# Rounding of the quantized activations moved from VectorE to ScalarE, 8 cores

## The chip, the cores and the metric

One Trainium2 chip, all 8 NeuronCores. The batch of 16 sequences is split over the cores, two sequences for each, and every core runs the same program on its own data without talking to the others. The metric is the device time in microseconds of the slowest core.

## The reference

One transformer layer of the post-norm kind with 1024 features, 16 heads and sequences of 2048 tokens. The feed-forward part is one matrix product on activations that are quantized to 8 bits.

```python
_d["L0_attn_x"]: (16, 2048, 1024) f32
...
scores = jnp.einsum('bhqd,bhkd->bhqk', Q, K) / jnp.sqrt(jnp.float32(dk))
scores = jnp.where(causal, scores, NEG)
m = jnp.max(scores, axis=-1, keepdims=True)
e = jnp.exp(scores - m)
attn = e / jnp.sum(e, axis=-1, keepdims=True)
out = jnp.einsum('bhqk,bhkd->bhqd', attn, V)
...
return out @ WO.T
...
ms = jnp.mean(jnp.square(x), axis=-1, keepdims=True)
x_norm = x * jax.lax.rsqrt(ms + EPS_RMS)
absmax = jnp.max(jnp.abs(x_norm), axis=-1, keepdims=True)
scale = 127.0 / jnp.clip(absmax, EPS_ACT, None)
x_q = jnp.clip(jnp.round(x_norm * scale), -128.0, 127.0) / scale
...
return jnp.einsum('bsd,od->bso', x_q, w_deq) + bias
...
x = _layernorm(x + _L0_attn_ref(x, L0_attn_WQ, L0_attn_WK, L0_attn_WV, L0_attn_WO), axis=-1)
x = _layernorm(x + _L0_ffn_ref(x, L0_ffn_w_int8, L0_ffn_weight_scale, L0_ffn_bias), axis=-1)
```

The part that matters here is `jnp.round`. The kernel does it by adding RC = 12582912 (1.5 times 2 to the 23rd) in f32 and taking it away again: at that size an f32 has no fraction bits, so the first addition rounds to a whole number.

## The kernel before

The kernel is written with an explicit queue for each engine. Functions append instructions and waits on semaphores to the lists of TensorE (PE, "t"), VectorE (DVE, "v"), ScalarE (ACT, "s"), GpSimd (POOL, "g") and SyncE (SP, "y"). Each engine runs its list in the order in which it was written, so an instruction that waits holds up all that stands behind it on that engine.

Each core handles its two sequences one after the other (`b` = 0, 1), in three stages:

- `ph1`: projections. Q and K are computed from the transposed input (matmuls L280, copied out by ACT at L290). V follows in groups at L325.
- `ph2`: causal attention. Scores (L388), exponential on ACT (L489 and L500), mask on POOL (L514), product with V (L406), normalization on DVE (L564) and transposes of the result (L432, L443).
- `ph45`: output projection, first norm, quantization, feed-forward product, second norm. It runs over 16 tiles of 128 tokens by 1024 features, in a software pipeline that is written out by hand. This is the stage of the change.

The steps of `ph45` for a tile t, by their names in the code:

- `emit_wo(t)`: 16 matmuls (L648) of the output projection into `psall`. `emit_xdma(t)` loads the residual into `xstg`.
- `VA(t)`, DVE: adds the residual (L678, z), takes maximum and minimum (L686, L689), mean and variance (L692 to L695), and a row of very small instructions on one column (L698 to L724).
- `SA(t)`, ACT: seven very small instructions (L733 to L751) that turn these into scales.
- `SB(t)`, ACT: writes the normalized tile `x1` in bf16 (L760).
- `VC(t)`, DVE: three passes over the tile: scale (L772, into `x1b`), round by adding RC and -RC (L777, in place), limit to -128..127 and write bf16 (L780, into `qint`).
- `G_x1pb(t)`, POOL: x1 plus bias into `x1b` (L790), after the quantization has read it.
- `T_qt_ffn(t)`: PE transposes `qint` (L803), ACT copies the result out (L816, `qT`), PE runs the 16 matmuls of the feed-forward product (L832).
- `VD(t)`, DVE: combines the product with x1 plus bias (L849), mean and variance (L857 to L870).
- `SD(t)`, ACT: two very small instructions (L882, L885) and the final norm (L889, `outst`). `G_out(t)`, POOL, issues the store (L902).

First come `emit_wo` of tiles 0 to 3, then tiles 0 and 1 with VA, SA, SB, VC, G_x1pb and T_qt_ffn, then VA and SA of tiles 2 and 3. After that the main loop runs for i = 0 to 15:

```python
VD(i)
...
if i + 4 < NP: emit_wo(i + 4)
SD(i, gps[i][0]); G_out(i, gps[i][0])
if i + 2 < NP: SB(i + 2); VC(i + 2); G_x1pb(i + 2); T_qt_ffn(i + 2)
if i + 4 < NP: ...; VA(i + 4, *gps[i + 4]); SA(i + 4)
```

So iterations 0 to 11 hold all steps, 12 and 13 have no new tile for `emit_wo` and `VA`, and 14 and 15 only finish. The accumulator of `emit_wo(i + 4)` is that which VD(i) has just read, so PE waits for L849 of VD(i).

During the `ph45` of the first sequence POOL also issues the loads for the second one (`preload_cb`). Behind VD(13) stand WQ (L965) and 7/8 of the input (L975); they wait for the feed-forward product of tile 13, and in POOL's queue they stand behind G_x1pb(14). Behind VD(15) stand WK (L984) and the rest of the input (L994). The `ph1` of the second sequence needs all of the input before its first matmul.

Of the kernel before, what the change touches and what calls it, by code (L numbers as in the profile page):

```python
# [10 lines left out]
AF = mybir.ActivationFunctionType  # L11
ALU = mybir.AluOpType
# [6 lines left out]
RC = 12582912.0  # L19
# [19 lines left out]
def build_nc():  # L39
# [13 lines left out]
    with ExitStack() as ctx:  # L53
# [27 lines left out]
        def small(name, shape, dtype):  # L81
            nonlocal o
            t = at(name, shape, dtype, o)
            nbytes = shape[1] * {F32: 4, BF16: 2, I32: 4}[dtype]
            o += (nbytes + 31) // 32 * 32
            return t
# [8 lines left out]
        rcol = small("rcol", [128, 1], F32)  # L95
        nrcol = small("nrcol", [128, 1], F32)
# [22 lines left out]
        sem_s = e(nc.semaphore("sem_s"))  # L119
        sem_v = e(nc.semaphore("sem_v"))  # L120
# [16 lines left out]
        def emit(engine, fn):  # L137
            ops[engine].append(fn)

        def bump(key, n=1):  # L140
            ctr[key] += n
            return ctr[key]

        def W(engine, key, val):
            if val is None or val <= 0:
                return
            sem = SEM[key]
            emit(engine, lambda eng, sem=sem, val=val: eng.wait_ge(sem, val))
# [442 lines left out]
        def ph45(b, trans_done, wo_done, w8_done, gpair, exp_last,  # L591
# [13 lines left out]
            ffnv = {}  # L605
            stats2v = {}
            appd2 = {}
            NP = 16

            def bufP(t):  # L610
# [2 lines left out]
            def zq(t):  # L613
                zt = z2 if (t % 4) < 2 else z2x
                return zt[:, (t % 2) * 1024:((t % 2) + 1) * 1024]
# [4 lines left out]
            def x1b2h(t):  # L620
                return x1b2[:, (t % 2) * 1024:((t % 2) + 1) * 1024]

            def qih(t):
                return qint2[:, (t % 2) * 1024:((t % 2) + 1) * 1024]
# [32 lines left out]
            def emit_xdma(t):  # L657
                gp = gpair[0]
                gpair[0] += 1
                W("y", "v", gpair[1].get(gp - 2))  # L660
                key = "xd" if t % 2 == 0 else "xd2"
                sem_x = SEM[key]
                def fd(eng, t=t, b=b, sem_x=sem_x):
                    src = ap(x_h, b * S * D + t * 128 * D, (D, 128), (1, D))
                    eng.dma_start(xh(t), src).then_inc(sem_x, 16)
                emit("y", fd)
                return gp, key, bump(key, 16)
# [61 lines left out]
            def SA(t):  # L729
                W("s", "v", statv[t])  # L730
                c0 = 14 * (t % 4)
                def f4(eng, t=t, c0=c0):
                    eng.activation(sc[:, c0 + 9:c0 + 11],  # L733
                                   sc[:, c0 + 2:c0 + 4], AF.Sqrt)
                    eng.activation(sc[:, c0 + 11:c0 + 12],
                                   sc[:, c0 + 1:c0 + 2], AF.Sqrt)
                    eng.drain()
                    eng.activation(sc[:, c0 + 6:c0 + 7],
                                   sc[:, c0 + 8:c0 + 9], AF.Identity,
                                   scale=sc[:, c0 + 9:c0 + 10])  # L740
                    eng.activation(sc[:, c0 + 7:c0 + 8],
                                   sc[:, c0 + 10:c0 + 11], AF.Identity,
                                   scale=127.0)
                    eng.activation(sc[:, c0 + 13:c0 + 14],
                                   sc[:, c0 + 11:c0 + 12], AF.Identity,
                                   scale=sc[:, c0 + 9:c0 + 10])
                    eng.drain()
                    eng.activation(sc[:, c0 + 12:c0 + 13],
                                   sc[:, c0 + 8:c0 + 9], AF.Identity,
                                   scale=sc[:, c0 + 7:c0 + 8])  # L750
                    eng.activation(w2a[:, t:t + 1],  # L751
                                   sc[:, c0 + 13:c0 + 14], AF.Identity,
                                   scale=wsb127[:, :]).then_inc(sem_s, 1)
                emit("s", f4)
                rsd[t] = bump("s")

            def SB(t):
                c0 = 14 * (t % 4)
                def f6(eng, t=t, c0=c0, z=zq(t)):
                    eng.activation(  # L760
                        x1[:, t * 1024:(t + 1) * 1024], z[:, :],
                        AF.Identity, bias=sc[:, c0 + 6:c0 + 7],
                        scale=sc[:, c0 + 9:c0 + 10]).then_inc(sem_s, 1)
                emit("s", f6)
                appd[t] = bump("s")

            def VC(t):
                W("v", "s", rsd[t])
                W("v", "t", qtmm_v.get(t - 2))
                c0 = 14 * (t % 4)  # L770
                def f7(eng, t=t, c0=c0, z=zq(t)):
                    eng.tensor_scalar(x1b2h(t), z[:, :],  # L772
                                      sc[:, c0 + 7:c0 + 8],
                                      sc[:, c0 + 12:c0 + 13],
                                      ALU.mult, ALU.add)
                    eng.drain()
                    eng.tensor_scalar(x1b2h(t), x1b2h(t), RC, -RC,  # L777
                                      ALU.add, ALU.add)
                    eng.drain()
                    eng.tensor_scalar(qih(t), x1b2h(t), 127.0,  # L780
                                      -128.0, ALU.min,
                                      ALU.max).then_inc(sem_v, 1)
                emit("v", f7)
                qv[t] = bump("v")

            def G_x1pb(t):
                W("g", "s", appd[t])
                W("g", "v", qv[t])
                def fg2(eng, t=t):
                    eng.tensor_tensor(x1b2h(t),  # L790
                                      x1[:, t * 1024:(t + 1) * 1024],
                                      bias_b2[:, 0:1024],
                                      ALU.add).then_inc(sem_m, 1)
                emit("g", fg2)
                x1pbv[t] = bump("g")
# [79 lines left out]
            def SD(t, gp):  # L875
                W("s", "v", stats2v[t])
                if gp >= 2:
                    _ok, _ov = outv[gp - 2]
                    W("s", _ok, _ov)
                c2 = 56 + 5 * (t % 2)  # L880
                def f15(eng, t=t, c2=c2, z=zq(t)):
                    eng.activation(sc[:, c2 + 2:c2 + 3],  # L882
                                   sc[:, c2 + 1:c2 + 2], AF.Sqrt)
                    eng.drain()
                    eng.activation(sc[:, c2 + 4:c2 + 5],  # L885
                                   sc[:, c2 + 3:c2 + 4], AF.Identity,
                                   scale=sc[:, c2 + 2:c2 + 3])
                    eng.drain()
                    eng.activation(  # L889
                        outst2[:, (t % 2) * 1024:(t % 2) * 1024 + 1024],  # L890
                        z[:, :], AF.Identity, bias=sc[:, c2 + 4:c2 + 5],
                        scale=sc[:, c2 + 2:c2 + 3]).then_inc(sem_s, 1)
                emit("s", f15)
                outrd[t] = bump("s")
# [18 lines left out]
            for t in range(2):  # L913
                gps[t] = emit_xdma(t)
                VA(t, *gps[t])
                SA(t)
                SB(t)
                VC(t)
                G_x1pb(t)
                T_qt_ffn(t)  # L920
            for t in (2, 3):
                gps[t] = emit_xdma(t)
                VA(t, *gps[t])
                SA(t)
            for i in range(NP):
                VD(i)
                if preload_cb is not None and i in (13, 15):
                    preload_cb(i, wo_y2v, ffnv)
                if i + 4 < NP:
                    emit_wo(i + 4)  # L930
                SD(i, gps[i][0])
                G_out(i, gps[i][0])
                if i + 2 < NP:
                    SB(i + 2)
                    VC(i + 2)
                    G_x1pb(i + 2)
                    T_qt_ffn(i + 2)
                if i + 4 < NP:
                    gps[i + 4] = emit_xdma(i + 4)
                    VA(i + 4, *gps[i + 4])  # L940
                    SA(i + 4)
# [8 lines left out]
        for b in range(BPC):  # L950
# [7 lines left out]
            def preload_cb(i, wo_y2v, ffnv, nxt=nxt, bn=b + 1):  # L958
# [19 lines left out]
                else:  # L978
# [19 lines left out]

            cb = preload_cb if b + 1 < BPC else None
            ph45(b, trans_done, wo_done, w8_done, gpair, exp_last,  # L1000
                 trans_ev, cb)
            pre = nxt if b + 1 < BPC else None
# [69 lines left out]
```

## Time and profile before

| | before |
|---|---|
| median of 3 runs | 1719.62 us (1715.51 to 1782.61) |
| profiled execution | 1719.22 us |
| its span (core 2, the slowest of 8) | 1717.6 us |
| spans of all cores | 1696.7 to 1717.6 us |
| busy: PE / ACT / DVE / POOL | 1242.3 / 831.5 / 575.8 / 306.0 us |

In all rows times count in microseconds from the start of the span. `ph45` runs from 626 to 854 for the first sequence and from about 1483 to the end for the second. In the rows the name `x1b` stands for the buffer x1b2, `z` and `z2x` for the two buffers of z, `x` for x1, and `128x1 f32` for the very small instructions on one column. A timeline row holds start, duration, engine, line, operation, output and input, and in brackets the idle time ahead of it and what ended it. A row of the windows holds the stretch, its length, the busy time (and the number of instructions) of PE's matmuls, PE's weight loads, DVE, ACT and POOL, then the granted clock of TensorE as a share of 2.4 GHz, the busy share of the DMA engines and the GB/s that they moved.

### The profile page before, as it was taken

The numbers are of one execution on the slowest core, as the hardware profiler recorded it, in microseconds if no ns is written. First come the engines' busy times: TensorE is split into PE (matmuls) and PEld (weight loads), VectorE is DVE, ScalarE is ACT, GpSimd is POOL, SyncE is SP. The second block draws the span as 40 slices with busy tenths as digits, with TensorE's granted clock in tenths as the row PEclk, the third lists the DMA queues.
The fourth block names the chain that finished last, engine by engine and source line by source line (L and its number), as shares of the span: only waits on it lengthen the run. The fifth ranks groups of instructions, "written<-read, shape, count | busy, mean of one in ns | idle before, by whom it ended". The sixth has DMA issues, their size and how long they took to land.

```text
span 1717.6 us, 25253 instructions; the slowest of 8 cores (1696.7 to 1717.6 us)
## 1 busy us (share of the span) xinstructions
PE 1242.3 (72%) x8710; PEld 586.3 (34%) x8710; DVE 575.8 (34%) x1647; ACT 831.5 (48%) x1188; POOL 306.0 (18%) x603
## 2 busy tenths in 40 slices
PE   1899777877777776676409997777777777756664
PEld 0344333443344332222204443334333434322222
DVE  1000322211111148888600012322211111488886
ACT  0232124777788743333303322156777888333333
POOL 1000222222211211221300002223222121111112
PEclk9999876567778888888759997765677787888887
DMA  9431102100000001222490220030000000012211
GB/s 157 64 50 20 30 1 32 19 1 2 1 2 1 1 13 62 86 78 83 92 177 1 50 48 3 1 50 1 1 2 1 1 2 1 25 64 84 74 62 62
DMA packets 23005, 64.54 MB, mean 38 GB/s; under 512 B 1379, under 2 KB 2403, under 8 KB 22884
## 3 DMA queue, kind: packets, MB, share of 16 engines
q0 software_dynamic: 18272, 46.14, 13.6%
q1 hardware_dynamic: 4612, 16.78, 3.2%
q8 instruction: 76, 1.25, 0.3%
q14 instruction: 45, 0.37, 0.1%
HBM read 75.50 MB, written 16.78 MB: 54 GB/s over the span
## 4 chain that ended last, share of the span: by engine, by line
PE 39%; ACT 21%; DVE 14%; POOL 10%; issue 9%; DMA 5%; DVEq 1%; ACTq 0%; POOLq 0%
ACT PT L489 20%; PE psall L280 13%; POOL PT L514 9%; PE psall L325 8%; PE psall L648 8%; PE psall L388 4%; PE psall L406 3%; DMA xT<-xt 3%; DMA wslotA<-wqt 3%; DVE dump L686 2%; DVE dumpb L689 2%; PE psall L432 2%; DVE st L692 1%; DVE st L693 1%; DVE z L849 1%
## 5 line engine op out<-in xcount | busy, mean ns | idle before, releaser
L489 ACT ACTIVATE PT<-psall,ebias 128x1024 bf16<-128x1024 f32 x448 | 468.3, 1116 | 309.5 <-PE psall L388 309.3
L388 PE MATMUL psall<-QT,KT 64*128 64x512 bf16 (+3 forms) x1280 | 282.3, 452 | 124.7 <-ACT PT L489 110.9
L406 PE MATMUL psall<-Vx,PT 128*128 128x65 bf16 x4352 | 304.4, 216 | 85.3 <-POOL PT L514 83.5
L514 POOL TENSOR_TENSOR PT<-PT,mask 128x128 bf16<-128x128 bf16 x512 | 200.9, 428 | 704.3 <-ACT PT L489 704.0
L406 PEld LDWEIGHTS psall<-Vx,PT 128*128 128x128 bf16 x4352 | 211.7, 110 | 248.3 <-issue 237.4
L551 DVE RECIPROCAL rinv<-psall 128x4 f32<-128x4 f32 x64 | 11.7, 182 | 636.5 <-PE psall L406 636.5
L648 PE MATMUL psall<-wslotA,OT 128*128 128x512 bf16 x512 | 159.1, 483 | 80.5 <-DVE z L849 44.5
L280 PE MATMUL psall<-xT,wslotA 128*128 128x512 bf16 x512 | 115.7, 390 | 88.9 <-DMA xT<-xt 52.6
L338 DVE CAST Vx<-psall 128x512 bf16<-128x512 f32 x64 | 44.2, 691 | 357.8 <-PE psall L325 356.5
L832 PE MATMUL psall<-wslotB,qT 128*128 128x512 bf16 x512 | 123.9, 398 | 42.1 <-ACT qT L816 42.1
L325 PE MATMUL psall<-wslotA,xT 128*128 128x512 bf16 x512 | 148.0, 460 | 0.0
L388 PEld LDWEIGHTS psall<-QT,KT 64*128 64x128 bf16 x1280 | 68.0, 97 | 225.7 <-issue 203.4
L500 ACT ACTIVATE PT<-psall,ebias 128x768 bf16<-128x768 f32 (+2 forms) x192 | 121.2, 697 | 0.0
L648 PEld LDWEIGHTS psall<-wslotA,OT 128*128 128x128 bf16 x512 | 59.3, 119 | 179.5 <-issue 151.0
L280 PE MATMUL psall<-xT,wslotB 128*128 128x512 bf16 x512 | 110.8, 379 | 0.0
L564 DVE TENSOR_SCALAR o_ring<-psall,rinv 128x64 bf16<-128x64 f32 x512 | 104.3, 277 | 5.8 <-issue 0.8
L280 PEld LDWEIGHTS psall<-xT,wslotA 128*128 128x128 bf16 x512 | 51.1, 100 | 154.7 <-issue 97.6
L832 PEld LDWEIGHTS psall<-wslotB,qT 128*128 128x128 bf16 x512 | 49.7, 101 | 106.5 <-issue 58.2
L325 PEld LDWEIGHTS psall<-wslotA,xT 128*128 128x128 bf16 x512 | 57.1, 114 | 83.2 <-issue 46.3
L733 ACT ACTIVATE sc<-sc 128x2 f32<-128x2 f32 x32 | 6.5, 204 | 159.0 <-DVE sc L724 159.0
L290 ACT CAST QT<-psall 128x512 bf16<-128x512 f32 x64 | 37.5, 586 | 91.3 <-PE psall L280 91.3
L790 POOL TENSOR_TENSOR x1b<-x,bias_b 128x1024 f32<-128x1024 bf16 x32 | 68.4, 2136 | 73.5 <-DVE qint L780 68.2
(98 smaller groups left out, 861.7 us busy)
## 6 DMA issues: line engine op xcount, KB each, us to landing
xstg<-x SPq DMA_DIRECT2D x32, 512.0 KB, 3.7
y<-outst POOLq DMA_DIRECT2D x32, 512.0 KB, 3.1
xT<-xt POOLq DMA_DIRECT2D x4, 1024.0 KB, 23.0
wslotA<-wqt POOLq DMA_DIRECT2D x2, 2048.0 KB, 31.4
wslotB<-wkt POOLq DMA_DIRECT2D x2, 2048.0 KB, 51.5
wslotA<-wvt POOLq DMA_DIRECT2D x2, 2048.0 KB, 17.2
wslotB<-w8t POOLq DMA_DIRECT2D x2, 2048.0 KB, 16.9
wslotA<-wot POOLq DMA_DIRECT2D x2, 2048.0 KB, 17.3
```

Of the source, the lines that this page charges most:

```text
L280: mm = eng.matmul(out, lhsT, rhs, start=(kt == 0), stop=(kt == 7), skip_group_check=True)
L325: mm = eng.matmul(out, lhsT, rhs, start=(kt == 0), stop=(kt == 7), skip_group_check=True)
L338: eng.tensor_copy(dst, src).then_inc(sem_v, 1)
L388: last = eng.matmul(out, lhsT, rhs, start=True, stop=True, skip_group_check=True)
L406: last = eng.matmul(out, lhsT, rhs, start=(i_glob < 2), stop=(i_glob >= n_total - 2), skip_group_check=True)
L489: eng.activation(PT[:, pt * 1024:(pt + 1) * 1024], psall[:, p * 1024:(p + 1) * 1024], AF.Exp, bias=ebias[:, :], scale=0.125).then_inc(sem_ ...
L500: eng.activation(dst, src, AF.Exp, bias=ebias[:, :], scale=0.125).then_inc(sem_s, 1)
L514: last = eng.tensor_tensor(blk, blk, mask01[:, :], ALU.mult)
L564: last = eng.tensor_scalar(o_ring[:, ro + qt * 1024 + h * 64: ro + qt * 1024 + h * 64 + 64], ps[:, qt * 65:qt * 65 + 64], rinv[:, s_ * 4 + ...
L648: mm = eng.matmul(out, lhsT, rhs, start=(dt == 0), stop=(dt == 7), skip_group_check=True)
L790: eng.tensor_tensor(x1b2h(t), x1[:, t * 1024:(t + 1) * 1024], bias_b2[:, 0:1024], ALU.add).then_inc(sem_m, 1)
L832: mm = eng.matmul(out, lhsT, rhs, start=(dt == 0), stop=(dt == 7), skip_group_check=True)
```

## The change

`VC(t)` is cut in three. DVE keeps the scaling pass and signals. ACT then does the rounding in two in-place passes over `x1b`, adding the columns `rcol` (RC) and `nrcol` (-RC), which were already there, with a drain between them (`SBr`). DVE then waits for ACT and does the limiting pass (`VC2`). The calls stand at the place of the old `VC` both times. In the changed kernel the scaling pass is L774, the two ACT passes are L785 and L788, the limiting pass is L797.

```diff
@@ -772,15 +774,30 @@
                     eng.tensor_scalar(x1b2h(t), z[:, :],
                                       sc[:, c0 + 7:c0 + 8],
                                       sc[:, c0 + 12:c0 + 13],
-                                      ALU.mult, ALU.add)
-                    eng.drain()
-                    eng.tensor_scalar(x1b2h(t), x1b2h(t), RC, -RC,
-                                      ALU.add, ALU.add)
-                    eng.drain()
+                                      ALU.mult,
+                                      ALU.add).then_inc(sem_v, 1)
+                emit("v", f7)
+                qvA[t] = bump("v")
+
+            def SBr(t):
+                W("s", "v", qvA[t])
+                def f7b(eng, t=t):
+                    eng.activation(x1b2h(t), x1b2h(t), AF.Identity,
+                                   bias=rcol[:, :], scale=1.0)
+                    eng.drain()
+                    eng.activation(x1b2h(t), x1b2h(t), AF.Identity,
+                                   bias=nrcol[:, :],
+                                   scale=1.0).then_inc(sem_s, 1)
+                emit("s", f7b)
+                rdone[t] = bump("s")
+
+            def VC2(t):
+                W("v", "s", rdone[t])
+                def f7c(eng, t=t):
                     eng.tensor_scalar(qih(t), x1b2h(t), 127.0,
                                       -128.0, ALU.min,
                                       ALU.max).then_inc(sem_v, 1)
-                emit("v", f7)
+                emit("v", f7c)
                 qv[t] = bump("v")
@@ -933,6 +952,8 @@
                 if i + 2 < NP:
                     SB(i + 2)
                     VC(i + 2)
+                    SBr(i + 2)
+                    VC2(i + 2)
                     G_x1pb(i + 2)
                     T_qt_ffn(i + 2)
```

The same two calls are added behind `VC(t)` for tiles 0 and 1.

On DVE, iteration 0 of the main loop of the first sequence, from the end of VD(0) to the start of VA(4), stood before as:

```order
L870 RECIPROCAL sc<-sc 128x1
L772 TENSOR_SCALAR x1b_57<-z2x,sc 128x1024
L777 TENSOR_SCALAR x1b_57<-x1b_57 128x1024
L780 TENSOR_SCALAR qint_58<-x1b_57 128x1024
L678 SCALAR_TENSOR_TENSOR z_53<-psall,xstg 128x1024
L686 TENSOR_SCALAR dump,sc<-z_53 128x1024
```

and stands now as:

```order
L887 RECIPROCAL sc<-sc 128x1
L774 TENSOR_SCALAR x1b_57<-z2x,sc 128x1024
L797 TENSOR_SCALAR qint_58<-x1b_57 128x1024
L680 SCALAR_TENSOR_TENSOR z_53<-psall,xstg 128x1024
L688 TENSOR_SCALAR dump,sc<-z_53 128x1024
```

The rounding pass is gone, L797 now waits for ACT, and VA(4) still stands directly behind it. On ACT the same iteration, with the waits, stands now as:

```order
L899 ACTIVATE sc<-sc 128x1 [waits sem_v]
L902 ACTIVATE sc<-sc 128x1
L906 ACTIVATE outst_61<-z_53,sc 128x1024
L762 ACTIVATE x_51<-z2x,sc 128x1024
L785 ACTIVATE x1b_57<-x1b_57,rcol 128x1024 [waits sem_v]
L788 ACTIVATE x1b_57<-x1b_57,nrcol 128x1024
L833 CAST qT<-psall 128x4x128 [waits sem_t]
```

Two passes have been put in behind the final norm of tile 0 (L906) and `x1` of tile 2 (L762), ahead of the copy of the transposed tile (L833).

## Rows read from the trace of the kernel before

**Rows 1.** Windows: the main loop of sequence one.

```profile
666.00:830.00 164.00, 112.62 (x480) 47.23 (x480) 136.48 (x322) 63.53 (x156) 32.57 (x24) 0.87 0.22 77
```

**Rows 2.** Chain in order of time (start, us, what), one iteration of the main loop.

```profile
775.92 1.29 DVE z L849
...
777.35 5.31 PE psall L648 x16
...
789.53 1.30 DVE z L849
```

**Rows 3.** Timeline of DVE, from the end of VD(i) to VA(i+4), the same iteration.

```profile
779.40 0.81 DVE L772 TENSOR_SCALAR x1b<-z2x,sc 128x1024 f32<-128x1024 f32 x1
780.29 0.69 DVE L777 TENSOR_SCALAR x1b<-x1b 128x1024 f32<-128x1024 f32 x1
781.06 0.69 DVE L780 TENSOR_SCALAR qint<-x1b 128x1024 bf16<-128x1024 f32 x1
782.89 1.23 DVE L678 SCALAR_TENSOR_TENSOR z<-psall,xstg 128x1024 f32<-128x1024 f32 x1 [1.14 <-PE psall L648]
```

**Rows 4.** Timeline of ACT, the same iteration.

```profile
780.18 1.24 ACT L889 ACTIVATE outst<-z,sc 128x1024 f32<-128x1024 f32 x1
781.32 1.23 ACT L760 ACTIVATE x<-z2x,sc 128x1024 bf16<-128x1024 f32 x1
```

**Rows 5.** The page, costliest groups: an ACT pass whose only column operand is the bias.

```profile
L489 ACT ACTIVATE PT<-psall,ebias 128x1024 bf16<-128x1024 f32 x448 | 468.3, 1116 | 309.5 <-PE psall L388 309.3
```

**Rows 6.** Timeline, tile 0: ACT hands over to DVE, then scale, limit, VA(1).

```profile
639.58 0.28 ACT L751 ACTIVATE w2a<-sc,wsb 128x1 f32<-128x1 f32 x1
639.76 1.23 ACT L760 ACTIVATE x<-z,sc 128x1024 bf16<-128x1024 f32 x1
...
639.96 0.81 DVE L772 TENSOR_SCALAR x1b<-z,sc 128x1024 f32<-128x1024 f32 x1 [2.96 <-ACT w2a L751]
...
641.62 0.69 DVE L780 TENSOR_SCALAR qint<-x1b 128x1024 bf16<-128x1024 f32 x1
642.23 1.22 DVE L678 SCALAR_TENSOR_TENSOR z<-psall,xstg 128x1024 f32<-128x1024 f32 x1
```

**Rows 7.** Timeline of DVE, starts of VD: 0, 1, 12; then 0, 1, 12, 15 of sequence two.

```profile
666.04 1.28 DVE L849 SCALAR_TENSOR_TENSOR z<-psall,w2a,x1b 128x1024 f32<-128x1024 f32 x1
680.37 1.28 DVE L849 SCALAR_TENSOR_TENSOR z<-psall,w2a,x1b 128x1024 f32<-128x1024 f32 x1
...
830.70 1.28 DVE L849 SCALAR_TENSOR_TENSOR z<-psall,w2a,x1b 128x1024 f32<-128x1024 f32 x1
...
1521.70 1.28 DVE L849 SCALAR_TENSOR_TENSOR z<-psall,w2a,x1b 128x1024 f32<-128x1024 f32 x1
1536.22 1.28 DVE L849 SCALAR_TENSOR_TENSOR z<-psall,w2a,x1b 128x1024 f32<-128x1024 f32 x1
...
1686.95 1.28 DVE L849 SCALAR_TENSOR_TENSOR z<-psall,w2a,x1b 128x1024 f32<-128x1024 f32 x1
...
1706.47 1.28 DVE L849 SCALAR_TENSOR_TENSOR z2x<-psall,w2a,x1b 128x1024 f32<-128x1024 f32 x1 [1.90 <-PE psall L832]
```

**Rows 8.** Timeline: POOL at the end of sequence one, PE's first matmul of sequence two.

```profile
837.54 2.13 POOL L790 TENSOR_TENSOR x1b<-x,bias_b 128x1024 f32<-128x1024 bf16 x1 [0.20 <-ACT x L760]
839.63 0.94 POOL L965 DMA_DIRECT2D wslotA<-wqt  x1
...
902.21 2.29 PE L280 MATMUL psall<-xT,wslotA 128*128 128x512 bf16 x5 [52.59 <-DMA xT<-xt]
```

**Rows 9.** Windows: the load for sequence two, columns as in rows 1.

```profile
860.00:870.00 10.00, 0.00 (x0) 0.00 (x0) 0.00 (x0) 0.00 (x0) 0.00 (x0) 0.50 1.03 158
```

**Rows 10.** Timeline: DVE's limiting pass of tile 14, and VD(14), sequence two.

```profile
1692.45 0.69 DVE L780 TENSOR_SCALAR qint<-x1b 128x1024 bf16<-128x1024 f32 x1
...
1701.10 1.28 DVE L849 SCALAR_TENSOR_TENSOR z2x<-psall,w2a,x1b 128x1024 f32<-128x1024 f32 x1 [2.21 <-PE psall L832]
```

**Rows 11.** Windows: one feed-forward product at the full granted clock, columns as in rows 1.

```profile
825.00:830.00 5.00, 3.61 (x16) 1.50 (x16) 4.29 (x13) 0.10 (x1) 0.73 (x1) 1.00 0.35 120
```

More of the change, by code:

```diff
@@ L607, in ph45 @@
             appd2 = {}
+            qvA = {}
+            rdone = {}
             NP = 16
@@ L918, in ph45 @@
                 VC(t)
+                SBr(t)
+                VC2(t)
                 G_x1pb(t)
```

## Prediction

> **What bounds the kernel now.** The change touches only `ph45`, so I read that stage. I began with its windows [rows 1]: in the 164 us between VD(0) and VD(12) of the first sequence DVE is busy 136.5 us (83%), PE 112.6, ACT 63.5, POOL 32.6. DVE is nearest to full, but no engine is full, so the order of the waits decides. The chain in order of time [rows 2] gives the cycle: VD's first pass L849 starts at 775.92 and frees an accumulator, PE runs the output projection (L648) from 777.35 to 782.66, DVE adds the residual at 782.89, and 6.64 us of statistics later the next L849 starts at 789.53. One iteration is 13.61 us. The scaling, rounding and limiting passes are not on this chain: the timeline of DVE [rows 3] shows them from 779.40 to 781.75, under the output projection, and then 1.14 us of idle time until PE is done. So the present cost of rounding in an iteration is nothing, and there is 1.14 us of room in front of L678. ACT [rows 4] is in the same stretch busy with the final norm L889 (from 780.18) and x1 (L760, 781.32 to 782.55).
>
> **What the change does to one iteration.** DVE loses L777, 0.69 us and a drain of 0.08 us (the gap to L780 at 781.06) [rows 3]. That alone would bring nothing, since L678 waits for PE until 782.89.
>
> ACT gets two passes. They stand behind L889 and L760 in its queue. L760 starts 1.14 us behind L889, so the next pass can start 1.14 us behind L760, at 782.46 [rows 4]. The scaled tile has then been ready since 780.21, so ACT's new wait costs nothing; the queue does.
>
> The trace of before has no in-place ACT pass with a bias column alone. The nearest rows bound it: L889 has f32 output and two column operands and takes 1.24 us [rows 4]; L489 has as many columns, a bias column and a constant scale like the new passes, but reads PSUM and writes bf16, 1.116 us [rows 5]. In rows 4 f32 output costs 0.01 us more than bf16. I take 1.13 us, near L489, whose operands are the same. The drain between them I take at 0.08 us, as on DVE. Both passes: 1.13 + 0.08 + 1.13 = 2.34 us, so the rounded tile is ready at 784.80.
>
> The handover to DVE takes 0.10 us (ACT's L751 ends at 639.86, L772 starts at 639.96), and VA's first pass follows the start of the limiting pass by 0.61 us (641.62 to 642.23) [rows 6]. So the limiting pass starts at 784.90, not 781.06, and L678 at 785.51, not 782.89. What is queued behind the waiting instruction on DVE is VA(i+4), and behind that the next VD: all of it moves by 2.62 us. The 1.14 us of idle time and the 0.77 us that were saved are already in this number. The iteration becomes 13.61 + 2.62 = 16.23 us.
>
> Who waits for DVE? The next output projection starts behind the next L849, and has until 785.51 instead of 782.89, so PE goes off the chain. Transposes, ACT's copy and the feed-forward product of the tile start behind the limiting pass, some 3.8 us later than before, but are needed only one iteration later.
>
> **Sum, against the profiled execution (1719.2 us, span 1717.6).**
> - Tiles 0 and 1. ACT is free at 640.90, 1.14 us behind L760, and sees the scaled tile (end 640.77 plus 0.10) at about 640.95. Then 2.34 + 0.10 + 0.61 gives VA(1) at 644.00 instead of 642.23 [rows 6], 1.77 us. Two tiles: 3.5 us for each sequence.
> - Iteration 0. It lasts 14.33 us in the first sequence and 14.52 in the second [rows 7], because a slower output projection holds L678 longer. That is covered now: 16.23 less these is 1.9 and 1.7 us.
> - Iterations 1 to 11: 11 x 2.62 = 28.8 us for each sequence. They average 13.67 us between 680.37 and 830.70 [rows 7]; what is above 13.61 I leave in both kernels.
> - The end of sequence one. Its tail does not count, because PE waits for the load of the next input until 902.21 [rows 8]. The load is issued when L790 of tile 14 ends (837.54 + 2.13, L965 at 839.63), which in iteration 12 follows the limiting pass. In the new order that pass ends 9.67 us behind VD(12) (784.90 + 0.69 - 775.92), L790 starts 0.15 us later, 9.82, against 6.84 before (837.54 - 830.70) [rows 7, 8]: 3.0 us. From there on the DMA engines are full (share 1.03 [rows 9]), so I let the whole load keep its 62.6 us from L965 to PE's first matmul. Sequence one: 3.5 + 1.9 + 28.8 + 3.0 = 37.2 us.
> - The end of sequence two. VD(15) needs the product of tile 15, which needs its limiting pass. VD(13) starts 9.59 us behind VD(12) (785.51 - 775.92, now without a wait for PE), the limiting pass of tile 15 ends 9.67 us after that, at 19.26. From the end of that pass to the VD of the same tile, transposes, copy and product took 7.95 us for tile 14 (1693.15 to 1701.10), which began after PE had been idle [rows 10]. That gives 27.2 us from VD(12) to VD(15) against 19.5 before [rows 7]; 0.4 of these 19.5 is a stall in issuing that I expect again, so 8.1 us. Sequence two: 3.5 + 1.7 + 28.8 + 8.1 = 42.1 us.
>
> Together 79.3 us. 1719.2 + 79.3 = 1798.5 us. The median of the runs, 1719.6, stands 0.4 us above that execution, which changes nothing: I say 1799 us.
>
> A rule that speaks against the change: the Trainium skill, page "ScalarE: Activation LUTs", section "Rules for kernel authors", says that additions belong on VectorE, which is faster for them. The trace agrees as to the price: one DVE instruction of 0.69 us does both additions, two ACT passes of over 1.1 us each replace it. But most of the 2.62 us is not the price: it is the place in ACT's queue.
>
> **Bounds.** If two passes overlap as L889 and L760 do (1.14 us apart at 1.24) and the drain costs nothing, two of 1.116 take 2.13 us, 0.2 less on 30 tiles: 6 us less, 1793. With 1.24 us each they take 2.56: 0.22 more on 30 tiles, 7 us, 1806. If the load's end hangs on its second part (issued behind VD(15)) instead of the first, the 3.0 us at the end of sequence one become 8, 5 us more.
>
> **Rivals.**
> 1. PE becomes the bound. The feed-forward product at granted clock 1.00, the 2.4 GHz level, takes 3.61 us [rows 11]; at 1.2 GHz it would be some 7 us, and so would L648, which takes 5.31 at present because the loop's mean clock is 0.87 [rows 1, 2]. The new order has PE idle behind L648 as well. If PE stayed at the low level throughout, transposes from 785.74, 1.1, copy 1.2, product 7 would end at about 795.0, the next L648 at 802.0, and L678 is due at 785.51 + 16.23 = 801.74. So it would be late by up to 0.5 us, on 24 iterations 12 us: 1811. Against it: the clock would have to be low in both products at once; with L648 alone low there is over 1 us to spare (777.35 + 7 = 784.35).
> 2. The load hides the first sequence. If the DMA engines were busy until 902 whatever `ph45` does, the 37.2 us would vanish: 1761 us. For it speaks PE's 52.6 us of waiting; against it, that POOL issues L965 only behind L790 of tile 14, so that the load is late by as much [rows 8].
> 3. Not slower: the relief of DVE counts and the wait does not. DVE is the busiest in the loop, and if the passes on ACT lay beside other work of DVE, up to 0.77 us on 32 tiles, 25 us, would be won: 1695. It decides whether the limiting pass can start by 782.28 (782.89 - 0.61). ACT is not even free before 782.46, so with passes of no length at all it would be late; only another order, with the rounding ahead of L889, or VA(i+4) ahead of the limiting pass, could do it, and the two queues printed with the change have neither. In a sentence apart: the Trainium skill, page "Perfetto Trace Analysis", section "Optimizing Scalar/DVE Operations", says that moving work to ScalarE may make sense where DVE is saturated, and by that rule the time would be this 1695; 83% with a wait for PE in each iteration [rows 1, 3] is not saturated.
> 4. The passes are hidden for the most part: if ACT took them as soon as the scaled tile is there (780.3), L678 would come at about 783.4, 0.5 us late, and with tiles 0 and 1 and the tails the sum is some 25 us: 1744, within 2%. Only if the instruction order were other than printed.
>
> **Chances.** The forecast with its bounds 0.80; rival 1 0.10; rival 2 0.05; rival 3 0.01; rival 4 0.02; the rest 0.02, half of it below 1685 and half above 1811. The first two hold 9 in 10, so the range is that of the forecast's bounds, from 1790 (a little under the lower one) to 1811, where the second part of the load or rival 1 would bring it. About 2% is what a measurement of this kernel can tell from no change, so between 1685 and 1754 is the same: rivals 3 and 4, 0.03. Faster is 0.01, half of the rest, and slower 0.96, the forecast with rivals 1 and 2 and the other half.
>
> **What would show it.** Right: in the main loop L849 follows L849 by about 16.2 us; L680 follows the start of L797 by 0.6 with no wait for PE; L797 waits for ACT's L788, about 4.7 us from the start of the wait; L785 starts 1.14 us behind L762; sequence one reaches its first projection matmul at about 939; the time outside `ph45` is unchanged. Wrong: L680 still waits for PE; L785 starts before L906; passes of much over 1.24 us, or an idle gap between them; an iteration under 15 us; or a changed length of the attention stage.

## The result and the profile after

| | before | after |
|---|---|---|
| median, 10 runs each | 1717.45 us | 1795.45 us |
| ratio | | 1.0455, 95% interval 1.0444 to 1.0467 |
| span of the profiled execution | 1717.6 us (core 2) | 1792.3 us (core 0) |

The change makes the kernel 4.55% slower, 78 us. The forecast was 1799 us with a range of 1790 to 1811. Some executions of either kernel were slower by a few per cent on one half of the chip; the ratio leaves them out.

The cycle of the main loop is read first. The timeline of DVE of the changed kernel, the iteration that answers to [rows 2, 3]:

```profile
782.76 1.28 DVE L866 SCALAR_TENSOR_TENSOR z2x<-psall,w2a,x1b 128x1024 f32<-128x1024 f32 x1
...
786.24 0.81 DVE L774 TENSOR_SCALAR x1b<-z,sc 128x1024 f32<-128x1024 f32 x1
791.75 0.69 DVE L797 TENSOR_SCALAR qint<-x1b 128x1024 bf16<-128x1024 f32 x1 [4.69 <-ACT x1b L788]
792.35 1.22 DVE L680 SCALAR_TENSOR_TENSOR z2x<-psall,xstg 128x1024 f32<-128x1024 f32 x1
...
798.98 1.28 DVE L866 SCALAR_TENSOR_TENSOR z<-psall,w2a,x1b 128x1024 f32<-128x1024 f32 x1
```

From L866 to L866 it is 16.22 us, against 13.61 before. L797 has waited 4.69 us for ACT. L680 follows the start of L797 by 0.60 us and no longer waits for PE, where before it was the one that waited, 1.14 us. The timeline of ACT for the same iteration [rows 4] shows what VectorE waits for:

```profile
787.02 1.24 ACT L906 ACTIVATE outst<-z2x,sc 128x1024 f32<-128x1024 f32 x1
788.16 1.22 ACT L762 ACTIVATE x<-z,sc 128x1024 bf16<-128x1024 f32 x1
789.29 1.13 ACT L785 ACTIVATE x1b<-x1b,rcol 128x1024 f32<-128x1024 f32 x1
790.50 1.15 ACT L788 ACTIVATE x1b<-x1b,nrcol 128x1024 f32<-128x1024 f32 x1
```

The scaled tile was ready at 787.05. The first rounding pass started at 789.29, when ACT was through with the norm and x1. Two passes of 1.13 and 1.15 us with a gap of 0.08, and 0.10 us until L797.

The timeline of PE for this iteration, and the windows of the main loop of sequence one (columns as in [rows 1]):

```profile
784.19 3.61 PE L650 MATMUL psall<-wslotA,OT 128*128 128x512 bf16 x15
792.59 1.01 PE L820 MATMUL psall<-ident,qint 128*128 128x128 bf16 x8 [4.78 <-DVE qint L797]
794.91 5.60 PE L849 MATMUL psall<-wslotB,qT 128*128 128x512 bf16 x13 [1.31 <-ACT qT L833]
```

```profile
668.00:864.00 196.00, 121.36 (x466) 50.30 (x476) 127.73 (x314) 89.84 (x180) 32.56 (x24) 0.77 0.19 65
```

The last row is that of a view that ends at 800; the product goes on to 801.15, 6.24 us in all. PE now has 4.8 us of idle time in the middle, between the output projection and the transposes. The granted clock of the loop fell from 0.87 to 0.77, but PE is off the chain, so it costs nothing: the output projection ends at 787.8 and is needed at 792.35.

The starts of VD, as in [rows 7]: 0, 1 and 12 of sequence one, then 0, 1, 12 and 15 of sequence two. Between them stand the issue of the load for sequence two (L986 was L965 before) and PE's first matmul as in [rows 8], and ahead of the last row the limiting pass of tile 15:

```profile
668.34 1.28 DVE L866 SCALAR_TENSOR_TENSOR z<-psall,w2a,x1b 128x1024 f32<-128x1024 f32 x1
684.51 1.28 DVE L866 SCALAR_TENSOR_TENSOR z<-psall,w2a,x1b 128x1024 f32<-128x1024 f32 x1
...
864.14 1.28 DVE L866 SCALAR_TENSOR_TENSOR z<-psall,w2a,x1b 128x1024 f32<-128x1024 f32 x1
...
876.07 0.94 POOL L986 DMA_DIRECT2D wslotA<-wqt  x1
...
935.58 57.69 PE L280 MATMUL psall<-xT,wslotA 128*128 128x512 bf16 x251 [44.80 <-DMA xT<-xt]
...
1558.34 1.28 DVE L866 SCALAR_TENSOR_TENSOR z<-psall,w2a,x1b 128x1024 f32<-128x1024 f32 x1
1574.57 1.28 DVE L866 SCALAR_TENSOR_TENSOR z<-psall,w2a,x1b 128x1024 f32<-128x1024 f32 x1
...
1754.60 1.28 DVE L866 SCALAR_TENSOR_TENSOR z<-psall,w2a,x1b 128x1024 f32<-128x1024 f32 x1
...
1773.17 0.69 DVE L797 TENSOR_SCALAR qint<-x1b 128x1024 bf16<-128x1024 f32 x1 [4.70 <-ACT x1b L788]
...
1781.41 1.28 DVE L866 SCALAR_TENSOR_TENSOR z2x<-psall,w2a,x1b 128x1024 f32<-128x1024 f32 x1 [4.16 <-PE psall L849]
```

Set against [rows 7, 8], in the order of the forecast's sum:

| term | forecast | measured |
|---|---|---|
| tiles 0 and 1, each sequence | 3.5 | 3.5 (first L678/L680 to VD(0): 35.9 to 39.4, sequence two) |
| iteration 0, sequence one / two | 1.9 / 1.7 | 1.8 / 1.7 (16.17 - 14.33, 16.23 - 14.52) |
| iterations 1 to 11, one / two | 28.8 / 28.8 | 29.3 / 29.3 (179.6 - 150.3, 180.0 - 150.7) |
| VD(12) to the load | 3.0 | 3.0 (11.93 - 8.93) |
| the load until PE's first matmul | 0 | -3.1 (59.5 instead of 62.6) |
| VD(12) to VD(15), sequence two | 8.1 | 7.3 (26.8 - 19.5) |

The start of `ph45` differs by 1.2 us between the two profiled cores, core 2 before and core 0 after: the first residual pass starts at 630.37 before and at 629.20 after. Projections and attention of sequence two are unchanged: 583.6 us before and 583.3 after, from the first matmul to the first residual pass. The measured terms add up to 76.3 us; less these 1.2 and 0.3 us it is the 74.7 us between the two spans. The medians are 78.0 us apart because the profiled execution before (1719.2) lies 1.8 us above its median and the one after (1794.1) 1.4 us below.

### The profile page after: what moved, and what is told of

It reads as the page before. It is cut to its first block, busy times and chain, and to the rows that moved or that the text cites. A ratio compares the mean times of both kernels' runs of the same rounds, so it can differ in the third digit from the quotient of the medians.

```text
span 1792.3 us, 25252 instructions; the slowest of 8 cores (1783.3 to 1792.3 us)
## 1 busy us (share of the span) xinstructions
PE 1264.2 (71%) x8645; PEld 595.4 (33%) x8710; DVE 551.0 (31%) x1615; ACT 900.9 (50%) x1252; POOL 305.6 (17%) x603
## 4 chain that ended last, share of the span: by engine, by line
PE 31%; ACT 23%; DVE 13%; issue 10%; POOL 9%; DMA 5%; DVEq 4%; ACTq 4%; POOLq 0%
ACT PT L489 18%; PE psall L280 13%; POOL PT L514 9%; PE psall L325 8%; PE psall L388 4%; ACTq L787 4%; PE psall L406 4%; DVEq L683 2%; DMA wslotA<-wqt 2%; DMA xT<-xt 2%; DVE dump L688 2%; ACT x1b L788 2%; DVE dumpb L691 2%; ACT x1b L785 2%; PE psall L432 2%
## 5 line engine op out<-in xcount | busy, mean ns | idle before, releaser
L849 PE MATMUL psall<-wslotB,qT 128*128 128x512 bf16 x498 | 179.6, 535 | 45.1 <-ACT qT L833 44.0
L325 PE MATMUL psall<-wslotA,xT 128*128 128x512 bf16 x493 | 142.8, 456 | 3.6 <-issue 3.0
L650 PE MATMUL psall<-wslotA,OT 128*128 128x512 bf16 x500 | 120.6, 395 | 18.4 <-DVE z L866 17.3
L820 PE MATMUL psall<-ident,qint 128*128 128x128 bf16 x256 | 29.2, 284 | 142.8 <-DVE qint L797 142.8
L849 PEld LDWEIGHTS psall<-wslotB,qT 128*128 128x128 bf16 x512 | 63.3, 128 | 153.5 <-issue 139.3
L650 PEld LDWEIGHTS psall<-wslotA,OT 128*128 128x128 bf16 x512 | 50.8, 101 | 85.8 <-issue 34.0
```

The costliest lines, as they stand in the source:

```text
L325: mm = eng.matmul(out, lhsT, rhs, start=(kt == 0), stop=(kt == 7), skip_group_check=True)
L650: mm = eng.matmul(out, lhsT, rhs, start=(dt == 0), stop=(dt == 7), skip_group_check=True)
L849: mm = eng.matmul(out, lhsT, rhs, start=(dt == 0), stop=(dt == 7), skip_group_check=True)
```

## The experiments

All runs below are compared with the kernel before on the same chip; ratios are to that.

**one_pass: half of the price.** Is the cost the passes themselves? One of the two is left out, so this kernel limits the scaled values without rounding them.

```diff
-                    eng.activation(x1b2h(t), x1b2h(t), AF.Identity,
-                                   bias=rcol[:, :], scale=1.0)
-                    eng.drain()
                     eng.activation(x1b2h(t), x1b2h(t), AF.Identity,
-                                   bias=nrcol[:, :],
+                                   bias=zcol[:, :],
                                    scale=1.0).then_inc(sem_s, 1)
```

Expected:

> The changed kernel with a single ACT pass that adds zero in place of the two rounding passes, so the values are limited but not rounded. Theory (the passes stand in a line behind the norm pass and x1 on ACT, and VectorE waits for the last): each tile loses one pass of 1.13 us and its gap of 0.07, so an iteration of the main loop takes 15.0 us instead of 16.2, and over 31 places on the path the time falls by 37 us from the changed kernel, to about 1758 us. Rival (the cost is the handing over between engines, not the passes): an iteration stays near 16 us and the time above 1785 us.

Measured: ratio 1.0239 (1.0223 to 1.0256). Against 1.0455 that is 0.0216 of 1715 us, 37 us, the number expected. The iteration is 15.01 us, in VD's starts in the timeline of DVE:

```profile
816.33 1.28 DVE L863 SCALAR_TENSOR_TENSOR z2x<-psall,w2a,x1b 128x1024 f32<-128x1024 f32 x1
831.34 1.28 DVE L863 SCALAR_TENSOR_TENSOR z2x<-psall,w2a,x1b 128x1024 f32<-128x1024 f32 x1
```

A pass on ACT goes into the time in full, 1.2 us for each place on the path. The handing over between engines is not what costs.

**round_first: the place in ACT's queue.** The rounding goes ahead of the final norm and of x1 in the main loop; tiles 0 and 1 stay as they are.

```diff
+                if i + 2 < NP:
+                    VC(i + 2)
+                    SBr(i + 2)
+                    VC2(i + 2)
                 SD(i, gps[i][0])
                 G_out(i, gps[i][0])
                 if i + 2 < NP:
                     SB(i + 2)
-                    VC(i + 2)
-                    SBr(i + 2)
-                    VC2(i + 2)
                     G_x1pb(i + 2)
```

Expected:

> The changed kernel with the two rounding passes ahead of the final norm of tile i and of x1 of tile i+2 in ACT's queue in the main loop (not for tiles 0 and 1). Theory (most of the cost is the place in the queue): the first pass starts 2.1 us earlier, an iteration takes 14.1 us (up to 14.5 if the delayed copy makes TensorE late), the time is about 1738 us, some 58 us below the changed kernel and 20 above the kernel before. Rival (the cost is the price of two ACT passes against one VectorE pass): nothing changes in the number or length of the passes, so the time stays at 1795 us.

Measured: ratio 1.0304 (1.0281 to 1.0326), 26 us less than the change where 58 were expected. The iteration is 15.27 us and not 14.1. The timeline, ACT and DVE in one iteration that starts with L866 at 724.10:

```profile
728.49 1.15 ACT L785 ACTIVATE x1b<-x1b,rcol 128x1024 f32<-128x1024 f32 x1 [2.82 <-DVE x1b L774]
...
730.96 0.69 DVE L797 TENSOR_SCALAR qint<-x1b 128x1024 bf16<-128x1024 f32 x1 [2.57 <-ACT x1b L788]
731.38 1.24 ACT L906 ACTIVATE outst<-z,sc 128x1024 f32<-128x1024 f32 x1
...
732.73 1.23 DVE L680 SCALAR_TENSOR_TENSOR z<-psall,xstg 128x1024 f32<-128x1024 f32 x1 [1.08 <-ACT outst L906]
```

The rounding came as early as the theory said: L797 starts 6.86 us behind L866 instead of 8.99. But L680 now waits for the final norm L906, which had been off the chain. There are four buffers of z (`z` and `z2x` hold two each), so VA(i+4) writes the one that the norm of tile i reads; with the norm behind the rounding in ACT's queue, that is the new last wait. The expectation had missed it. The rival, no change at all, is excluded.

**round_first_z: that wait taken away.** Two more buffers of z, in the space of PT.

```diff
+        z2y = at("z2y", [128, 2048], F32, OFF_PT)
...
-                zt = z2 if (t % 4) < 2 else z2x
+                zt = (z2, z2x, z2y)[(t % 6) // 2]
...
-                W("v", "s", outrd.get(t - 4))
+                W("v", "s", outrd.get(t - 6))
```

Expected:

> round_first with six buffers for z instead of four (the two more in the space of PT, which this stage does not use), VA(i+4) waiting for the final norm of tile i-2 instead of tile i. Theory (in round_first the gain of the earlier rounding was cut by a new wait, VA for the final norm that still reads the buffer of z that VA writes): that wait goes, the residual pass follows the start of the limiting pass by 0.6 us, an iteration takes 14.1 us instead of 15.3, and 24 iterations make it 27 us faster than round_first, about 1.014 of the kernel before, 1737 us where that takes 1713. Rival (TensorE or ACT's delayed copy sets the pace there): an iteration stays above 15 us and the ratio at 1.03.

Measured: ratio 1.0140 (1.0125 to 1.0156). The iteration is 14.10 us:

```profile
796.15 1.28 DVE L867 SCALAR_TENSOR_TENSOR z2x<-psall,w2a,x1b 128x1024 f32<-128x1024 f32 x1
...
824.70 1.28 DVE L867 SCALAR_TENSOR_TENSOR z2y<-psall,w2a,x1b 128x1024 f32<-128x1024 f32 x1
838.80 1.28 DVE L867 SCALAR_TENSOR_TENSOR z<-psall,w2a,x1b 128x1024 f32<-128x1024 f32 x1
```

With the order in ACT's queue and the buffer put right, the same two passes cost 1.4% instead of 4.55%: 24 us of 78. The better place in the queue is thus worth 54 us. That doesn't divide the loss into two thirds for the place and one third for the passes, since by one_pass a single pass is worth 37 us when the queue is left as it is. The rows show why the two overlap. The limiting pass could start 2.07 us behind the end of the scaling pass (782.28, from rival 3, less 780.21) before L678 would be late. The queue ahead of the passes takes 2.24 us, the passes take 2.36 and the handover 0.10, which makes 4.70 us, 2.6 too many. The passes alone make L678 late by 0.5 us, as this run shows. The queue alone would make it late by some 0.3; that is an estimate from the same numbers, and no run shows it.

**limit_late: VectorE never waits for the rounding.** The other order of rival 3.

```diff
                     SBr(i + 2)
-                    VC2(i + 2)
-                    G_x1pb(i + 2)
-                    T_qt_ffn(i + 2)
                 if i + 4 < NP:
                     gps[i + 4] = emit_xdma(i + 4)
                     VA(i + 4, *gps[i + 4])
+                if i + 2 < NP:
+                    VC2(i + 2)
+                    G_x1pb(i + 2)
+                    T_qt_ffn(i + 2)
+                if i + 4 < NP:
                     SA(i + 4)
```

Expected:

> The changed kernel with the limiting pass of tile i+2 (and what hangs on it: bias sum, transposes, copy, feed-forward product) behind VA(i+4) instead of ahead of it in the main loop, so that VectorE never waits for the rounding. Theory: transposes, copy, product and the next output projection then form one line behind the limiting pass, 9.5 to 12.5 us, and VA another 6.6, so an iteration takes 17 to 20 us and the time is 1800 to 1880 us. Rival (the relief of VectorE counts): an iteration of 12.8 to 13.6 us, 1695 to 1717 us.

Measured: 1852.2 us, a single run, with the kernel before at 1713, and within the 1800 to 1880 expected. The iteration averages 19.3 us (VD(1) at 682.98, VD(12) at 895.25, 11 iterations). The timeline of one of them, DVE and PE:

```profile
702.14 0.69 DVE L797 TENSOR_SCALAR qint<-x1b 128x1024 bf16<-128x1024 f32 x1
...
705.30 5.01 PE L849 MATMUL psall<-wslotB,qT 128*128 128x512 bf16 x16 [1.31 <-ACT qT L833]
710.15 3.62 PE L650 MATMUL psall<-wslotA,OT 128*128 128x512 bf16 x16
714.01 1.23 DVE L680 SCALAR_TENSOR_TENSOR z2x<-psall,xstg 128x1024 f32<-128x1024 f32 x1 [6.97 <-PE psall L650]
```

The wait for ACT is gone and one of 6.97 us for PE stands in its place: feed-forward product and output projection are now one line behind the limiting pass. DVE was spared its wait and nothing was won, because the limiting pass that was put back is the one that PE waits for.

**load_early: what the load for sequence two hangs on.**

```diff
-                if preload_cb is not None and i in (13, 15):
-                    preload_cb(i, wo_y2v, ffnv)
+                if preload_cb is not None and i in (12, 14):
+                    preload_cb(i + 1, wo_y2v, ffnv)
```

Expected:

> The changed kernel with the loads for sequence two issued one iteration earlier in GpSimd's queue (the first part ahead of the output and the bias sum of iteration 12, the second ahead of those of iteration 14). Theory (the load is a transfer at full DMA share whose end moves with its issue): the first issue moves from 876 to about 866 us, the first projection matmul of sequence two as much, 10 us less in total, about 1785 us. Rival (the end of the load hangs on its second part or on the end of the stage): no change, 1795 us, or less than 3 us.

Measured: ratio 1.0391 (1.0372 to 1.0409), 0.0064 of 1715 us below the change: 11 us. The timeline of POOL shows the load of WQ (L986) issued 4.3 us ahead of VD(12) (862.38 there) instead of 11.9 behind it, and that of the input (L996) 2.4 us behind it, when tile 13's product is done, instead of 12.9 us (877.00 - 864.14):

```profile
858.08 0.94 POOL L986 DMA_DIRECT2D wslotA<-wqt  x1
864.74 2.87 POOL L996 DMA_DIRECT2D xT<-xt  x4 [5.71 <-PE psall L849]
...
890.48 2.88 POOL L1015 DMA_DIRECT2D xT<-xt  x4
...
917.90 57.01 PE L280 MATMUL psall<-xT,wslotA 128*128 128x512 bf16 x256 [28.94 <-DMA xT<-xt]
```

From the issue of L986 to PE's first matmul it is 59.8 us, as in the change (59.5), so the matmul comes 15.9 us earlier against VD(12). That is more than the 10 expected, as L986 moved by 16.2. The median moved by 11 us only: the profiled execution (1775.4 us) lies 4 us below the three others (1779.6 to 1779.8), and what these lose is open. The last part of the input (L1015) is issued 28.1 us behind VD(12) in both kernels (892.24 - 864.14 in the change), so the end of the load does not hang on it. So the end of sequence one is set by the issue of the first loads and not by the end of the stage, as the forecast's sum had it, and rival 2 of the prediction is excluded as well: the load does move.

**early_vd: what bounds the kernel before.** Rounding stays on VectorE. VD is cut behind its first pass, VA too, and the first pass of VD(i+1) goes ahead of the statistics of VA(i+4). The main part of the edit:

```diff
                     VA(i + 4, *gps[i + 4])
+                if i + 1 < NP:
+                    VD(i + 1)
+                if i + 4 < NP:
+                    VAs(i + 4)
                     SA(i + 4)
```

Here `VA` and `VD` are the first passes (L678, L849) and `VAs`, `VDs` what followed them; the iteration begins with `VDs(i)`.

Expected:

> The kernel before (rounding on VectorE) with one edit of order: the first pass of VD(i+1), which frees the accumulator that the next output projection waits for, stands directly behind the first pass of VA(i+4) instead of behind its statistics. Theory (the chain of before is VA, the first pass of VD and the output projection, and VectorE's own work is only 12.5 us of its 13.6): the output projection then runs beside the statistics, the wait of 1.1 us goes, an iteration takes 12.5 us, 24 of them 26 us less, a ratio of 0.985. Rival (TensorE cannot keep up, feed-forward product and output projection in a line at a mean clock below full): an iteration of 13 us or more, ratio 0.99 to 1.01.

Measured: ratio 0.9825 (0.9809 to 0.9842), 30 us faster than the kernel before; the iteration is 12.41 us, with a longer one now and then:

```profile
694.92 1.22 DVE L678 SCALAR_TENSOR_TENSOR z2x<-psall,xstg 128x1024 f32<-128x1024 f32 x1
696.38 1.28 DVE L855 SCALAR_TENSOR_TENSOR z2x<-psall,w2a,x1b 128x1024 f32<-128x1024 f32 x1 [0.24 <-issue]
...
707.33 1.22 DVE L678 SCALAR_TENSOR_TENSOR z2x<-psall,xstg 128x1024 f32<-128x1024 f32 x1
```

No wait for PE is left in the loop. VectorE's own work is the bound now, so in such a kernel moving some of it to ACT may pay; the next runs try it.

**new_order_dve and new_order_act: the same rounding where the passes lie beside other work.** Both use one order for DVE and ACT, and the early load. The main loop of new_order_act, without its conditions and loads:

```python
emit_wo(i + 4)
VC2(i + 2); G_x1pb(i + 2); T_qt_ffn(i + 2)
VA(i + 4); VD(i + 1)
VC(i + 3); SBr(i + 3)
VDs(i + 1); SD(i + 1); G_out(i + 1); SB(i + 3)
VAs(i + 4); SA(i + 4)
```

The scaling pass thus stands over 7 us ahead of the limiting pass. new_order_dve differs in that the rounding is a VectorE pass directly ahead of the limiting one:

```diff
-                    eng.activation(x1b2h(t), x1b2h(t), AF.Identity,
-                                   bias=rcol[:, :], scale=1.0)
-                    eng.drain()
-                    eng.activation(x1b2h(t), x1b2h(t), AF.Identity,
-                                   bias=nrcol[:, :],
-                                   scale=1.0).then_inc(sem_s, 1)
...
+                    eng.tensor_scalar(x1b2h(t), x1b2h(t), RC, -RC,
+                                      ALU.add, ALU.add)
+                    eng.drain()
```

Expected of new_order_dve:

> Rounding on VectorE, with a new order: first pass of VA(i+4), first pass of VD(i+1), scaling pass of tile i+3, statistics of VD(i+1) and final norm, statistics of VA(i+4), rounding and limiting of tile i+3; the loads for sequence two issued early as in load_early. Theory: VectorE is the bound with 12.4 us of work for an iteration; with 10 us from the load the ratio is 0.975. It is the partner of new_order_act, so that rounding on VectorE and on ACT stand in the same order.

Expected of new_order_act:

> new_order_dve with the rounding on ACT as in the change: the scaling pass stands some 7 us ahead of the limiting pass, so that both ACT passes lie beside VectorE's statistics. Theory (the change is slow because nothing lies beside the passes, not because of the engine that does them): the limiting pass waits for nothing, VectorE is relieved of 0.77 us, an iteration takes 11.7 us if TensorE keeps up, the prologue still pays 1.8 us for each of tiles 0 and 1, and the time is 10 to 13 us below new_order_dve, a ratio near 0.968. Rival 1 (TensorE becomes the bound at 12.4 us or more): no faster than new_order_dve, up to 7 us slower. Rival 2 (two ACT passes cost time wherever they stand): slower than the kernel before.

Measured: 0.9774 (0.9757 to 0.9790) for new_order_dve, 0.9732 (0.9694 to 0.9769) for new_order_act. The intervals overlap, so these two runs alone don't decide between them. The timeline of new_order_act shows the mechanism: the two ACT passes are done at 729.29, the limiting pass starts at 734.01 and waits for nothing:

```profile
726.01 0.81 DVE L779 TENSOR_SCALAR x1b<-z,sc 128x1024 f32<-128x1024 f32 x1 [0.17 <-issue]
...
726.92 1.15 ACT L790 ACTIVATE x1b<-x1b,rcol 128x1024 f32<-128x1024 f32 x1 [2.45 <-DVE x1b L779]
728.14 1.15 ACT L793 ACTIVATE x1b<-x1b,nrcol 128x1024 f32<-128x1024 f32 x1
...
734.01 0.69 DVE L803 TENSOR_SCALAR qint<-x1b 128x1024 bf16<-128x1024 f32 x1
```

An iteration of new_order_dve takes 12.38 us (VD at 706.72 and 719.10), those of new_order_act 11.52 us and some 12.2 us in turns (VD at 700.79, 712.31, 724.56). In the longer ones the residual pass waits for PE:

```profile
723.10 1.23 DVE L680 SCALAR_TENSOR_TENSOR z<-psall,xstg 128x1024 f32<-128x1024 f32 x1 [0.64 <-PE psall L650]
```

Rival 1 thus holds in part: PE is next. A short iteration is 0.86 us shorter than that of new_order_dve, a long one some 0.2, so PE takes back some 0.35 us of the 0.86 on average.

**new_order_mix and new_order_dve2: the pair again on one chip.** new_order_dve2 is new_order_dve once more. new_order_mix keeps the rounding of tiles 0 and 1 on VectorE.

```diff
                 SB(t)
-                VC(t)
-                SBr(t)
-                VC2(t)
+                VCdve(t)
```

`VCdve` is the `VC` of the kernel before.

Expected of new_order_mix:

> new_order_act with the rounding of tiles 0 and 1 of each sequence left on VectorE, where nothing lies beside it, and on ACT for the 14 others. Theory (ACT rounding pays where the passes lie beside VectorE's work and costs where they don't): 4 times 1.8 us, 7 us below new_order_act, a ratio near 0.969, and 10 to 14 us below new_order_dve on the same chip. Rival (TensorE sets the pace in new_order_act, so what VectorE is spared in an iteration is lost again): within 4 us of new_order_dve, ratio 0.975 or more.

Expected of new_order_dve2:

> new_order_dve once more, as the partner of new_order_mix on the same chip in the same rounds: a ratio of 0.976 to 0.979 as before.

Measured: 0.9721 (0.9709 to 0.9734), 1665.5 us, and 0.9777 (0.9764 to 0.9789), 1676.1 us. The intervals don't touch: in this order, with tiles 0 and 1 left on VectorE, rounding on ACT is 9.6 us faster by the ratios (0.0056 of 1714) and 10.5 by the medians, at the lower edge of the 10 to 14 expected. The 7 us expected against new_order_act can't be read from the runs; the interval of that kernel is too wide. new_order_mix is the fastest version of the case, 2.8% below the kernel before and 7% below the change.

## Why the prediction was right

**What bounds.** The forecast read 1.14 us of room in front of L678 and put the quantization off the chain. early_vd confirms the chain (VA, first pass of VD, output projection): the one edit that cuts it gives 30 us.

**The step of one iteration.** 2.62 us forecast, 2.61 measured. Each part of it stood: ACT's queue (first pass 2.24 us behind the scaled tile, forecast 2.25), the passes (1.13 and 1.15, forecast 1.13 each), the gap (0.08), the handover (0.10), the start of VA (0.60, forecast 0.61). The prediction's remark that most of the 2.62 us is the place in the queue and not the price of the passes was only argued, and holds by half. The better place takes off 2.12 us of an iteration (16.22 to 14.10), but leaving out one of the two passes takes off 1.21 with the queue as it is. The two fill the same 2.07 us of room, and the sum needed neither share. For tiles 0 and 1 the recorded 640.95 should read 640.90 (640.77 + 0.10 is 640.87, and ACT is free at 640.90); tile 0 came out 1.72 us longer, from L762 to L680, where 1.77 was forecast.

**The sum.** 79.3 us forecast, 78.0 measured between the medians, 74.7 between the two spans. Two terms were off. For the load the forecast kept 62.6 us, and the profiled core of the changed kernel took 59.5. That is a matter of the core: over all eight, from L965 or L986 to the first matmul they take 58.1 to 62.6 us before (mean 60.2) and 58.4 to 61.4 after (mean 59.4). At the end of sequence two the step from the limiting pass to VD of the same tile was set at 7.95 us, that of tile 14 before, and took 7.5 for tile 15, 0.4 us less, and the stall in issuing did not recur. Against these, iterations 1 to 11 came out 0.5 us longer in each sequence, and by the spans the forecast is 4.6 us too long. That it comes within 1.3 us of the difference of the medians is in part luck, since it started from an execution that lay 1.8 us above its median.

**The rivals.** 1 (PE becomes the bound): the clock did fall, to 0.77, but from iteration 1 on only the feed-forward product was slow, the output projection took 3.61 us, and DVE had no wait for PE between 680 and 864; excluded by the timeline. 2 (the load hides sequence one): excluded, by the table above and by load_early. 3 (relief of DVE): excluded; of the two orders that it named, limit_late is 8% slower than before and round_first 3%. The rule of the Trainium skill, page "Perfetto Trace Analysis", section "Optimizing Scalar/DVE Operations", that such a move may make sense where DVE is saturated, is borne out once its condition is met: 4.55% slower where DVE waited for PE (83% busy), 0.56% faster where DVE was the bound (90% busy in the loop of new_order_dve, 22.26 of 24.75 us), the passes lay beside its work and tiles 0 and 1 stayed on DVE. 4 (passes taken at once): not this order, but round_first is nearly that case; its sum in the prediction, 25 us, is what round_first_z measured (24 us), and needs the extra buffers of z which rival 4 had not thought of.

## What to carry to other kernels

A pass that is moved to another engine in the middle of a dependent row costs as much as the queue ahead of it there and its own length together exceed the room that the row has. Read what is ahead of it there, and what is behind the instruction that waits for its result on the old engine. Here moving it paid only where the old engine was the bound, and where the pass was issued so far ahead of its use that other work of the old engine lay between. When an order in a queue is put right, ask which buffer is now read later than before: here the gain of an earlier rounding was halved by a norm that still held its input.

## What was not expected of the hardware

TensorE's slow level moved from one product to the other. Before, the output projection took 5.31 us [rows 2], at a mean granted clock of 0.67 from 777.3 to 782.5, and the feed-forward product 3.61 at 1.00 (784.4 to 788.1). After, the output projection takes 3.61 at 1.00 (784.2 to 787.8) and the feed-forward product 6.24 at 0.55 (794.9 to 800.9; it lies between 4.6 and 6.4 us in the loop of sequence one). In each kernel the product that follows the longer idle time of the engine is the slow one: 2.94 us of idle time stood ahead of the output projection before, while after it 4.8 us stand ahead of the transposes and the feed-forward product. In new_order_act the feed-forward product took 3.61 us in one iteration, where the transposes followed the output projection at once, and 6.46 in the next, where PE had waited 3.18 us for the limiting pass. Its iterations alternate between 12.2 and 11.5 us: the output projection behind the slow product is late for the residual pass. What sets the level was not tested further.
